# One accumulator in place of two for the softmax denominators of a gated cross-attention and expert kernel

## The reference

```python
lat = layer_norm(latents); ctx = layer_norm(context)
q = (lat @ Wq).reshape(b, n, 16, 64); k, v = split(ctx @ Wkv); k = apply_rope(k, cos, sin)
attn = einsum('bhnd,bhsd->bhns', q, k) * scale
attn = clip(attn, -11, 11)
attn = softmax(attn, axis=-1)
out = einsum('bhns,bhsd->bhnd', attn, v)
return out @ Wo + bo
```

## Time and profile before

| | us |
|---|---|
| median of 3 runs | 1250.18 |
| lowest, highest | 1249.36, 1250.47 |
| the profiled execution, its time | 1251.45 |
| the profiled execution, its span | 1249.7 |
| TensorE, VectorE, ScalarE, GpSimd busy | 1200.6, 1007.3, 578.9, 399.9 |

### The profile page before, as it was taken

One profiled execution on the slowest core, in us unless ns is written; L12 is line 12 of the kernel. 1 busy time (PEld: TensorE's weight loads), 2 busy tenths in 40 slices (PEclk: granted clock), 3 DMA queues, 4 the chain that ended last, 5 costly groups with the idle time before them and its releaser, 6 DMA issues.

```text
span 1249.7 us, 22921 instructions
## 1 busy us (share of the span) xinstructions
PE 1200.6 (96%) x8289; PEld 813.3 (65%) x8289; DVE 1007.3 (81%) x1688; ACT 578.9 (46%) x1044; POOL 399.9 (32%) x409
## 2 busy tenths in 40 slices
PE   5799999999999999999999999989999999999997
PEld 3555555564555655555555555555899999999896
DVE  7699999988999898899989899997685664665554
ACT  4554567555556655455755554554322222222221
POOL 5333664433376333346534334552100000000000
PEclk9999999999999999999999999999999999999999
DMA  7000000000000000010000000022011020000001
GB/s 194 1 9 27 18 27 10 18 10 11 18 24 29 10 9 10 11 34 23 13 10 17 15 10 9 9 77 85 1 34 35 1 67 0 1 1 0 18 17 34
DMA packets 33070, 29.65 MB, mean 24 GB/s; under 512 B 9144, under 2 KB 31808, under 8 KB 32960
## 3 DMA queue, kind: packets, MB, share of 16 engines
q1 hardware_dynamic: 32944, 28.21, 7.3%
q10 hardware_dynamic: 16, 0.00, 0.0%
HBM read 26.11 MB, written 2.10 MB: 23 GB/s over the span
## 4 chain that ended last, share of the span: by engine, by line
PE 80%; DVE 11%; issue 3%; POOL 3%; ACT 1%; SPq 0%; DMA 0%; POOLq 0%; DVEq 0%; ACTq 0%
PE pv L1230 14%; PE sc L1216 12%; PE kv L1161 5%; PE kv L1163 5%; PE kv L1162 5%; PE sc L1161 5%; PE sc L1162 5%; PE sc L1163 5%; PE mi L1161 4%; PE mi L1163 3%; PE mi L1162 3%; DVE acc L827 3%; PE tr L1202 3%; PE mi L1240 2%; PE pv L1161 1%
## 5 line engine op out<-in xcount | busy, mean ns | idle before, releaser
L632 ACT ACTIVATE prob<-sc 128x1024 f32<-128x1024 f32 x256 | 249.1, 1029 | 221.8 <-PE sc L1216 219.1
L1230 PE MATMUL pv<-prob,val 128*32 128x512 f32 x2048 | 247.1, 600 | 2.7 <-DVE prob L812 2.7
L493 POOL TENSOR_TENSOR rot_s<-k_raw,sinb 128x256 f32<-128x256 f32 x128 | 107.3, 838 | 388.6 <-ACT k_raw L580 388.6
L1216 PE MATMUL sc<-q_hid,big 64*128 64x512 f32 x1536 | 212.7, 409 | 4.7 <-issue 4.7
L1216 PEld LDWEIGHTS sc<-q_hid,big 64*128 64x128 f32 x1536 | 134.3, 184 | 113.2 <-issue 60.0
L812 DVE TENSOR_SCALAR prob<-prob 128x1024 f32<-128x1024 f32 x256 | 183.3, 728 | 27.7 <-ACT prob L632 23.9
L827 DVE TENSOR_TENSOR acc<-acc,prob 128x1024 f32<-128x1024 f32 x128 | 204.9, 1621 | 0.0
L1082 DVE TENSOR_SCALAR q_hid<-prob,gb 128x512 fp32r<-128x512 f32 x128 | 62.6, 489 | 104.8 <-ACT prob L713 103.6
L497 POOL TENSOR_TENSOR rot_c<-rot_c,rot_s 128x256 f32<-128x256 f32 x128 | 124.7, 974 | 35.2 <-DVE rot_c L801 19.0
L1230 PEld LDWEIGHTS pv<-prob,val 128*32 128x32 f32 x2048 | 56.8, 109 | 112.3 <-issue 82.7
L713 ACT ACTIVATE prob<-sc,b1t 128x512 f32<-128x512 f32 x64 | 44.1, 689 | 171.0 <-PE sc L1163 171.0
(11 more groups left out here) (170 smaller groups left out, 2432.7 us busy)
## 6 DMA issues: line engine op xcount, KB each, us to landing
val<-in_L_ffn_w SPq DMA_DIRECT2D x6, 1024.0 KB, 5.1
rows<-in_ctx SPq DMA_DIRECT2D x32, 128.0 KB, 2.1
w_raw<-in_L_xattn_Wq SPq DMA_DIRECT2D x16, 256.0 KB, 2.7
w_raw<-in_L_xattn_Wo SPq DMA_DIRECT2D x64, 64.0 KB, 1.9
prob<-in_L_xattn_Wkv SPq DMA_DIRECT2D x8, 256.0 KB, 4.8
xacc<-in_x SPq DMA_DIRECT2D x4, 512.0 KB, 4.6
val<-in_L_ffn_w SPq DMA_DIRECT2D x4, 512.0 KB, 3.8
out<-xacc SPq DMA_DIRECT2D x4, 512.0 KB, 2.9
```

What stands on the lines that cost most here:

```text
L493: g.tensor_tensor(rot_s[:].rearrange("p (h a c) -> p h a c", h=4, a=2), kh[:, :, ::-1, :], sinb[:, t].unsqueeze(1).to_broadcast([P, 4, 2, ...
L632: a.activation(prob[:, s % 2, i, :], sc[i][:], ACT.Exp, scale=DH ** -0.5).then_inc(exp_done[i], 1)
L1216: last = mm(sc[i][:, h * N:(h + 1) * N], kst[rows_h, u % 2, j, lk, t * P:(t + 1) * P], q_sp[rows_h, p % 2, lq, :], start=lk + lq == 0, sto ...
L1230: last = mm(pv[g * 32:(g + 1) * 32, :], val[:, u % 2, 2 * c + i, at:at + 32], prob[:, s % 2, i, h * N:(h + 1) * N], start=c == 0 and i == ...
```

## The change

There is one accumulator `acc` of 1024 columns and one semaphore `summed`. At c == 0 and i == 1 it is written as the sum of the two tiles of that step; every later step adds both tiles to it, one after the other. That makes seven additions per pair, each of which waits for the one before. The first waits for `den_ready`. `denominators` waits for all seven and multiplies the one accumulator: 4 calls. Exp waits for the count at which the tile that it overwrites has been added; for c == 2 that is the addition of c == 0.

```diff
-        acc = sb("acc", [2, 2 * N])
+        acc = sb("acc", [2 * N])
...
-        summed = [sem("summed0"), sem("summed1")]
+        summed = sem("summed")
...
-                wait(act, summed[i], q * 3 + (-1, 0, 1, 1)[c])
+                wait(act, summed, q * 7 + ((-3, -2), (-1, 0), (1, 1), (2, 3))[c][i])
...
-                if c == 0:
+                if c == 0 and i == 0:
                     return
                 dve.wait_ge(clamped[i], step_no(b, u, s) + 1)
-                if c == 1:
+                if c == 0:
                     wait(dve, den_ready, q)
-                    v.tensor_tensor(acc[:, i, :], prob[:, 0, i, :], prob[:, 1, i, :], ALU.add).then_inc(summed[i], 1)
+                    v.tensor_tensor(acc[:], prob[:, 0, 0, :], prob[:, 0, 1, :], ALU.add).then_inc(summed, 1)
                 else:
-                    dve.wait_ge(summed[i], q * 3 + c - 1)
-                    v.tensor_tensor(acc[:, i, :], acc[:, i, :], prob[:, s % 2, i, :], ALU.add).then_inc(summed[i], 1)
+                    dve.wait_ge(summed, q * 7 + 2 * c - 1 + i)
+                    v.tensor_tensor(acc[:], acc[:], prob[:, s % 2, i, :], ALU.add).then_inc(summed, 1)
...
             def denominators(b, p):
-                for i in range(2):
-                    pe.wait_ge(summed[i], (pair_no(b, p) + 1) * 3)
-                    for g in range(4):
-                        half, h = g // 2, g % 2
-                        at = h * N + half * QH
-                        last = mm(mi[g * 32:(g + 1) * 32, 0:QH], ones[:, 0:32], acc[:, i, at:at + QH],
-                                  start=i == 0, stop=i == 1)
+                pe.wait_ge(summed, (pair_no(b, p) + 1) * 7)
+                for g in range(4):
+                    half, h = g // 2, g % 2
+                    at = h * N + half * QH
+                    last = mm(mi[g * 32:(g + 1) * 32, 0:QH], ones[:, 0:32], acc[:, at:at + QH], start=True, stop=True)
                 last.then_inc(den_ready, 1)
```

More of the change, by code:

```diff
@@ L134, in flamingo_kernel @@
         f_rows = lat_r[:]
-        b2b = acc[:, 0, :].rearrange("p (e d) -> p e d", e=E)
+        b2b = acc[:].rearrange("p (e d) -> p e d", e=E)
         xt_raw = l_aff[:]
```

## The result

The change runs in 1268.64 us (median of 4 runs, 1267.23 to 1271.50) against 1249.77 us for the kernel before: ratio 1.0154, 95% interval 1.0134 to 1.0175, so 19 us slower. The forecast was 1272.4 us in 1254 to 1284. The profiled execution took 1271.50 us (span 1269.7, before 1249.7).

A forecast was written before the change was run, and what follows sets the result against it. TensorE sets the pace, VectorE in places; the addition makes VectorE bind. Terms 13.9 + 8.5 + 0.5 - 0.7 = +22.2 us on the profiled 1251.45 give 1273.6, less 1.27 to the median 1272.4; range 1254 to 1284.

The forecast's parts named there:

- 63.9 us of idle time: VectorE's idle time over three loop turns (18.94 us each) and the last six pairs (7.10), against 63.5 us of new work.
- The new sum at 1.72 us: VectorE's added sum per pair, beside GpSimd's rotation addition: 1.72 us start to start, 1.14 at the low end.
- pairs 4 and 5: Pairs that also normalise the next context: 4.04 us of new VectorE work less 1.55 of waiting, +2.49 us per turn.
- The chain's 0.15 us: VectorE's gap where a sum waits for the one before: 0.15 us, three times per odd pair, once per even.
- The matmul's 16.0 us at most: TensorE's saving from half the ones-matmul: 8 of 16 records, 0.50 us per pair, 32 pairs, 16.0 us at most.
- The ledger of one turn: Place-by-place count over one loop turn of eight head pairs: +4.62 us, +13.9 us for three turns.
- pairs 7 and 0: Pair 7 into 0: VectorE's lag reaches `q_low`, for which `project` waits; +1.72 us per turn.
- The last six pairs: With the residual's statistics on VectorE: 10.96 us of new work less 2.5 us of usable idle time, +8.46 us.
- The stretch before the loop: The second pair of the kernel, +0.5 us.
- The early release: Exp of step 2 finds its buffer free after step 0, not step 1: -0.7 us, between 0 and -2.6.
- The rival that GpSimd becomes the bound: New sum holds GpSimd's rotation work 1.1 us, costing some 0.5 us more in each of 32 pairs: 1288 us; 10%.
- The rivals of a faster and of an unchanged kernel: Faster: TensorE keeps the pace, addition hides, 1234 us, 5%. Unchanged: exp of step 2 ahead gives back all 22.2, 1250, 4%.

## Why the prediction was right, point by point

**The direction and the mechanism** held: the addition, which with its side effects brought 50.0 us of VectorE work, met idle time that couldn't all be used, and the named waits appeared: `project` on `q_low`, the denominators on the last sum, `values` on `normalise`. The size was 19.2 us (16.7 to 21.9) for 22.2. The 63.9 us of idle time were a little too many: they take the second turn for all three, while the three turns before the change have 18.0, 19.4 and 16.2 us (cut at L832), 60.6 us with the last six pairs.

**The new sum at 1.72 us** was too long. From its start to that of the next instruction it took 1.45 us on average: in 12 of the 32 pairs (pair 3 of every batch, pairs 4 and 5 of three each, pairs 6 and 7 of the last) it took 1.13 to 1.14 us, the low end, and its record is 1.21 to 1.23 us long, which the prediction gave as a sign of being wrong. In the other 20 it took 1.56 to 1.72 us. The row that I took holds where VectorE's sum and GpSimd's addition start together. In pair 0 VectorE comes later, the addition starts 0.18 us ahead of the sum, and 1.56 us are left. In all the sums were 46.5 us for the forecast's 53.9.

**The chain's 0.15 us** measured 0.12 to 0.13 at one place, and the chain as a whole 3.5 us. The Trainium skill, VectorE: DVE Perf Modes, "The DRAIN you can't avoid", has the semaphore cost nothing extra, measured on copies; for two additions of which the second is made to wait for the first, the run shows 0.12 us.

**The matmul's 16.0 us at most**: alone 5.1. I had TensorE's saving as used up in pairs 2 and 3; it was kept there in the second and third turn (-0.90 and -0.89 for a forecast of 0), as in the run with the half matmul alone (-0.89). In return I had not priced that the half that went had filled the wait for the last sum, though I named that first half as now waiting.

**The ledger of one turn**, forecast and measured in the second turn: pairs 2 and 3, 0 and -0.90; pairs 4 and 5, +2.49 and +1.98; pair 6, +0.91 and +0.99; pairs 7 and 0, +1.72 and +1.69; pair 1, -0.50 and -0.43; together +4.62 and +3.33. The places where a queue could be followed to one wait (`q_low` before `project`) came out within 0.1 us, and the third turn repeats them (+0.97 and +1.71). For three turns the forecast was +13.9 and the traces have +12.5, of which 6.2 in the first. That pairs 4 and 5 came out near is in part luck: my +2.49 took two sums of 1.72 us, and they took 1.13; in their place stand the longer L478 (+0.96) and, in this turn, a lower clock (below). In the third turn, at full clock, they grew by 0.78 only. Nor is L478 the whole of it: in the run with the new addition behind the reciprocals it is back at 1.01 us, and pair 4 still grows by 0.75, with L497 at 1.52 us.

**The last six pairs**, +8.46, grew by 5.2: 6.8 up to the start of the last pair, of which that pair gave 1.6 back. They had more slack than the 2.5 us I allowed, and in 4 of the 6 the new sum took 1.13 or 1.14 us, where I had that in the last two alone. **The stretch before the loop**, +0.5, grew by 3.5; what it waits for there was not tested. These two misses nearly cancel, which is luck. Together, by place: 12.5 + 5.2 + 3.5 less 1.2 in the expert part is 20.0 us between the two profiled executions, for a forecast of 22.2.

**The early release**, 0.7, measured 2.6 with an interval that takes in zero.

**The rival that GpSimd becomes the bound** was named for the rotation, at 16 us; the traces show it for L478 in one pair of eight, at most some 3 us in all (0.96 in each of three turns). The mechanism was real and its place was another. The rivals of a faster and of an unchanged kernel fall with the extra addition's run.

Left open: the single parts don't quite make up the whole. The run with the early release undone is the addition, the half matmul and the chain together, and costs 21.9 us; the addition and the half matmul in one run (+14.8) and the chain (+3.5) add up to 18.3. The 3.6 us between them lie just outside their intervals (by them 0.8 to 6.4). So the chain may cost more once VectorE is full, and it has one more link with seven additions; no run separates this.

## What to carry to other kernels

Half-hidden work on a pacing engine may be cover for a wait: price what the saving stands in front of, not its length. When an engine at 90% is the one that gets new work, count its idle time in each stretch between two waits that bind it to the pacing engine (here `q_low` before `project`); the average says only whether it could fit. And a step can cost by its place alone: moving one of six additions forward, with nothing added, was 5 to 6 us slower here.

## What the runs showed of the hardware

A sum with both operands in SBUF and a GpSimd instruction hold each other up in either order. Where GpSimd's addition L497 starts first (467.22 us, the sum at 467.40), the sum takes 1.64 us for 1.21 alone. Where the sum starts first, a GpSimd instruction of only 4 numbers per partition, the power of L478, takes 1.97 us for 1.01. The Trainium skill, SBUF — State Buffer, "Who interferes with whom", says that the later one waits for the first to end; the 0.96 us fit that, since the sum of 352.98 ends 1.08 us after the power's start.

TensorE's clock fell behind the wait for the rotation that follows. Windows of the changed kernel (granted clock third from the end), and TensorE's timeline there:

```profile
356.50:364.00 7.50, 5.23 (x43) 2.82 (x44) 7.36 (x18) 2.64 (x5) 6.81 (x11) 1.00 0.22 70
364.00:367.50 3.50, 3.50 (x13) 2.27 (x15) 2.53 (x6) 1.45 (x4) 1.99 (x4) 0.51 0.02 5
```
```profile
362.73 0.44 PE L1202 MATMUL tr<-ident,rot_c 128*128 128x128 f32 x2 [2.27 <-POOL rot_c L497]
```

TensorE had sat idle for 2.27 us, went on at the full 2.4 GHz for 1.4 us and then ran 3.4 us at half of it, 1.2 GHz, its matmuls 0.43 us apart in place of 0.23. The same pair one turn earlier, with a wait of 2.28 us, did so too (granted clock 0.74 between 150 and 155 us); one turn later, again with 2.28 us, it kept the full clock, and the pair grew by 1.09 in place of 2.27 us by the ruler. The kernel before has such a dip as well, behind the 2.34 us at one jump of the loop. So a like wait is followed by the lower clock in some places and not in others, and a stretch read in one execution can hold 1 us or more of it. The mean clock doesn't explain the scatter between executions: the four runs of the change go with it (0.992, 0.993, 0.987 and 0.987 at 1267.2, 1267.6, 1269.6 and 1271.5 us), but with the early release undone the run at 0.993 took 1274.3 us and the one at 0.984 took 1269.6.
